# Reordering the first two and last three images, and moving one accumulation bank from the maxima to the first products

## The chip, the cores and the metric

The kernel runs on one core of a Trainium2 chip. Its engines are TensorE (PE: matmuls, and PEld: its weight loads), VectorE (DVE), ScalarE (ACT), GpSimd (POOL) and SyncE (SP: DMA issue). Each runs its own stream of instructions in order, and they meet at semaphores. The metric is the device time in microseconds (us), a median over runs; lower is better. Accumulation memory has eight banks, each holding 128 x 512 float32 values. The kernel uses all eight.

## The reference, cut to what matters

The input is x, 8 images of 32 x 32 positions with 96 channels. For each image, 1024 tokens of 96 values:

```
x = x + moe_a(groupnorm(x))            # 8 experts, hidden 384, gates = softmax over the top 2 of 8
t = x + attention(layernorm(x))        # 6 heads of 16, causal, over all 1024 tokens, with projection
out = t + moe_c(layernorm(t))          # 4 experts, hidden 384, top 2 of 4, gates renormalised
```

Both mixtures compute every expert for every token: h = gelu(x @ W1[e] + b1[e]), y = h @ W2[e], and the sum of gate[e] * y + b2.

## The kernel before, in words

**Splitting.** Float32 operands are cut into a high and a low float16 half, and a product is three matmuls (high x high, low x high, high x low). Weights are scaled by 64 and cut once, at the start, in six parts of two experts each (`split_w1`, `split_w2`, lines 1215 to 1224): VectorE writes the high half and then the low one (`split`, line 1059). The same function cuts the gate's and the attention weights.

**Groups and slots.** A group is one expert on one chunk of 512 tokens: 16 groups for the first mixture of an image (2 chunks x 8 experts), 8 groups for the last one. A group has four slots. In slots 0 to 2 TensorE multiplies the chunk with a third of W1 into a bank `ps_u` (`first_layer`, nine matmuls in three slots); ScalarE applies gelu twice, to float32 `hid` and to float16 `hidh` (lines 951, 952); GpSimd subtracts and writes the low half `hidl` (line 637). One group later, TensorE multiplies by W2 into a bank `ps_y` (`second_layer`, one block of 128 tokens a slot), and VectorE combines with the gates into `acc`, four instructions at a time (`combine`, line 1133). There are two banks `ps_u` and two banks `ps_y`. A first product waits until ScalarE has read the bank that it writes: `h_ready` at all but one of the products before (line 711).

**Attention.** The rows' maxima are found first. For each head and block of 128 queries there are one or two score products into the banks `ps_r`, of which there are three, and a VectorE reduction of each (`maximum`, lines 790 and 1178); 72 of them per image. A score product waits until the reduction three before is done (line 798). Then the maxima are transposed, cut into halves and written by DMA as extra rows of q (`maxima`), and in the softmax stage of 24 steps TensorE computes the transposed scores again with the maximum subtracted, into the five banks `ps_r` and `ps_u` in turn, ScalarE exponentiates, GpSimd clears the future on the diagonal, and TensorE multiplies with the values. Sums of rows go through DRAM by DMA and come back spread over partitions (`rb`), which VectorE multiplies into `yt`.

**Iterations.** Iteration `it` runs, in this order on every engine, the groups of image `it`'s first mixture (phase 0), the groups of image `it - 2`'s last mixture (phase 1), and image `it - 1`'s softmax (phase 2). `schedule(it)` places all other work, called chores, by phase and slot: loading and normalising the next image (`x_load`, `x_turn`, `gn_*`), the routing (`logits`, `exp`, `route`, `gates`, `bias`), the maxima (`max`), and the chain behind attention (`sum_inverse`, `normalise_y`, `project`, `ln2`, `x2_turn`). All engines walk the same table, each doing its own part of a chore; a chore stands in its engine's queue ahead of what follows it.

Iterations 2 to 7 have all three parts. Iterations 0 and 1 have no last mixture, and 0 no softmax. Iteration 8 has no groups: it runs the 72 maxima of image 7 in the slots of phase 0, with nothing beside them but the end of image 6's attention, and then image 7's softmax. Iteration 9 runs the last mixture of image 6, iteration 10 that of image 7. In full iterations 56 of the maxima lie in phase 0 and 16 in phase 1.

**The start.** GpSimd sets all constants (lines 564 to 593) and raises `zeroed`, for which VectorE's first instruction (line 1212), the first group mean and SyncE's remaining weight loads wait. The group-normalised operand of every image is `xah`, `xal`; so image 1's can be written only after image 0's last first product.

Of the kernel before, what the change touches and what calls it, by code (L numbers as in the profile page):

```python
# [26 lines left out]
P = 128  # L27
NIMG, T, D = 8, 1024, 96
TT = T // P
CH = 512  # L30
# [50 lines left out]
def walk(iteration):  # L81

    for it in range(FIRST_LOOP):
        iteration(it, True, it >= 1, it >= 2)
    for it in range(FIRST_LOOP, NIMG):
        iteration(it, True, True, True)
# [5 lines left out]
def image_c(it):  # L92

    return Image(it, -3 if isinstance(it, int) and it > NIMG else -2)
# [61 lines left out]
def maxima_at(first, last, n0, n1):  # L156
# [11 lines left out]
ROUTE_C_LATE = [(0, "route_c", 0), (0, "route_c", 1), (1, "route_c", 2), (1, "route_c", 3), (4, "gates_c", 0),  # L168
                (5, "bias_c", 0), (6, "bias_c", 1)]
# [5 lines left out]
              (10, "gates_a", 0), (20, "bias_a", 0), (22, "bias_a", 1), *FRONT)  # L175
MAX_A = 56


def schedule(it):

    if isinstance(it, int) and it == 0:
        first = [(0, "split_w2", 0), (1, "route_a", 0, 0), (1, "route_a", 1, 0), (1, "route_a", 2, 0),
                 (2, "split_w1", 1), (3, "gates_a", 0, 0), (4, "bias_a", 0, 0), (5, "bias_a", 1, 0),
                 (6, "split_w2", 1), (7, "x_load", 0)]
        first += [(8 + 2 * n, ("split_w1", "split_w2")[n % 2], 2 + n // 2) for n in range(2 * W1_PARTS - 4)]
        first += [(25 + n, "turn_watt", n) for n in range(3)] + [(29 + n, "turn_wp", n) for n in range(2)]
        first += [(32 + 2 * n, "zero", n) for n in range(ZEROS)]
        return placed(*first, *GN), placed((0, "gn_apply", 0)), placed()
    if isinstance(it, int) and it == 1:

        first = [(0, "logits_a", 0, 0), (0, "exp_a", 0, 0), (1, "route_a", 0, 0), (1, "route_a", 1, 0),
                 (2, "route_a", 2, 0), (4, "gates_a", 0, 0), (5, "bias_a", 0, 0), (6, "bias_a", 1, 0),
                 (7, "ln1", 0, -1), (8, "ln1", 1, -1), (8, "x_load", 0), (11, "ln1_apply", 0, -1),
                 (12, "ln1_apply", 1, -1)]
        first += [(14 + 2 * n, "x1_turn", n, -1) for n in range(NC)] + [(18 + 2 * n, "qk", n, -1) for n in range(2 * NC)]
        return (placed(*first, (26, "val", 0), (28, "val", 1), (29, "keep_x1", 0),
                       *maxima_at(32, SLOTS_A - 1, 0, MAXU), *GN),
                placed(*GN_LATE, (3, "maxima", 0)), SOFT)
    if isinstance(it, int) and it == NIMG:

        return (placed(*VALUES, (16, "sum_inverse", 0), (34, "normalise_y", 0), (35, "normalise_y", 1),
                       (37, "project", 0), (40, "project", 1), (41, "keep_x1", 0),
                       *maxima_at(3, SLOTS_A - 1, 0, MAXU)),
                placed((0, "maxima", 0)),
                placed((0, "ln2", 0), (1, "ln2", 1), (4, "ln2_apply", 0), (5, "ln2_apply", 1), (6, "x2_turn", 0),
                       (8, "x2_turn", 1), (11, "logits_c", 0), (12, "exp_c", 0), (13, "route_c", 0),
                       (14, "route_c", 1), (15, "route_c", 2), (16, "route_c", 3), (21, "gates_c", 0)))
    if isinstance(it, int) and it == NIMG + 1:

        return (placed(),  # L210
                placed((1, "bias_c", 0, -3), (4, "bias_c", 1, -3), (5, "sum_inverse", 0), (14, "normalise_y", 0),
                       (15, "normalise_y", 1), (16, "project", 0), (18, "project", 1), (19, "ln2", 0),
                       (20, "ln2", 1), (25, "ln2_apply", 0), (26, "ln2_apply", 1), (28, "x2_turn", 0),
                       (30, "x2_turn", 1)),
                placed((0, "store", 0, -3)))
    if isinstance(it, int) and it == NIMG + 2:

        return (placed(),
                placed((0, "logits_c", 0, -3), (0, "exp_c", 0, -3),
                       *((slot, name, unit, -3) for slot, name, unit in ROUTE_C_LATE)),  # L220
                placed((0, "store", 0, -3)))
# [7 lines left out]
PROLOGUE = ["split_gate", "x_turn", "x_turn", "gn_stats", "gn_mean", "gn_spread", "split_w1", "gn_apply", "logits_a",  # L229
            "exp_a"]  # L230
# [9 lines left out]
Group = namedtuple("Group", "moe c e")  # L240


def rounds(moe_a, moe_c):

    groups = [Group(0, c, e) for c in range(NC) for e in range(EA)] * moe_a
    groups += [Group(1, c, e) for c in range(NC) for e in range(EC)] * moe_c
    if not moe_a:  # L250
        yield None, None, 0, range(SLOTS_A)
    for n, (up, down) in enumerate(zip(groups + [None], [None] + groups) if groups else ()):
        phase, g = (0, n) if moe_a and n < GA + (not moe_c) else (1, n - GA * moe_a)
        yield up, down, phase, range(TC * g, TC * (g + 1))
    if not moe_c:
        yield None, None, 1, range(SLOTS_C)
# [10 lines left out]
def prologue(m, chore):  # L267

    for n, name in enumerate(PROLOGUE):
        run_chores(m, chore, [(name, n - 1 if name == "x_turn" else 0, Image(0, 0))])  # L270
# [7 lines left out]
def build(nc, x, cWg, cbg, cW1, cb1, cW2, cb2, w_attn, b_attn, w_proj, b_proj,  # L278
          fWg, fbg, fW1, fb1, fW2, fb2, out):
    nc.disable_value_cache = True  # L280
    with ExitStack() as ctx:
# [109 lines left out]
        ps_u = [ctx.enter_context(nc.psum_tensor(f"ps_u{i}", [P, CH], F32)) for i in range(2)]  # L391
        ps_y = [ctx.enter_context(nc.psum_tensor(f"ps_y{i}", [P, CH], F32)) for i in range(2)]
        ps_r = [ctx.enter_context(nc.psum_tensor(f"ps_r{i}", [P, CH], F32)) for i in range(3)]
        ps_m = ctx.enter_context(nc.psum_tensor("ps_m", [P, CH], F32))

        def operand_c(b):

            last = isinstance(b.value(1, 0), int) and b.value(1, 0) == NIMG - 1
            return (xah, xal) if last else (xch, xcl)
# [12 lines left out]
        zeroed = sem("zeroed")  # L412
        zeroed_late = sem("zeroed_late")
        consts = sem("consts")
        ident_ready = sem("ident_ready")
        wg_ready = sem("wg_ready")
        w1_ready = sem("w1_ready")
# [41 lines left out]
        def _(sp):  # L459
# [26 lines left out]
            for part in range(2, W1_PARTS):  # L486
                load_w1(part)
                load_w2(part)
            sp.dma_start(watt[:], w_attn.rearrange("(s o) i -> o s i", s=3)).then_inc(watt_loaded, 16)
# [57 lines left out]
            def iteration(it, moe_a, attend, moe_c):  # L547
                for _, _, phase, slots in rounds(moe_a, moe_c):
# [12 lines left out]
        def _(pool):  # L561
# [9 lines left out]
            for tile, value in ((epsilon, 1e-5), (power, -0.5), (minus, -1.0), (ra.gates, 0.0), (rc_.gates, 0.0),  # L571
                                (rc_.prob, -1.0), (b2a, 0.0), (b2c, 0.0), (wpad, 0.0)):
                g.memset(tile[:], value)
            pool.drain()
            for tile, value in ((identb, 0.0), (mask_q, 0.0), (mpart, NEG), (mtop, 0.0)):
                g.memset(tile[:], value)
            pool.drain()
            for tile, value in ((xah, 1.0), (xal, 0.0), (xbh, 1.0), (xbl, 0.0), (xch, 1.0), (xcl, 0.0)):
                g.memset(tile[ONE:ONE + 1, :], value)
# [7 lines left out]
                            pattern=[[3, D // 3], [0, 3]], channel_multiplier=-1)  # L587
            pool.drain().then_inc(zeroed, 1)
            g.affine_select(out=identb[:], in_=identb[:], compare_op=ALU.not_equal, fill=1.0, base=0,
                            pattern=[[-1, P]], channel_multiplier=1)  # L590
            g.affine_select(out=mask_q[:], in_=mask_q[:], compare_op=ALU.is_ge, fill=NEG, base=0,
                            pattern=[[-1, P]], channel_multiplier=1)
            pool.drain().then_inc(consts, 1)
# [36 lines left out]
            def iteration(it, moe_a, attend, moe_c):  # L630
                for up, _, phase, slots in rounds(moe_a, moe_c):
# [17 lines left out]
            for name in PROLOGUE:  # L649
                chore(name, 0, Image(0, 0))  # L650
# [3 lines left out]
        def _(pe):  # L654
# [52 lines left out]
            def first_layer(it, group, j):  # L707

                xh, xl = (xah, xal) if group.moe == 0 else operand_c(image_c(it))
# [4 lines left out]
                bank = ps_u[(HT * grp.k + j) % 2]  # L714
# [666 lines left out]
```

## Time and profile before

| | us |
|---|---|
| Median of 3 runs | 1399.39 (1399.3 to 1401.2) |
| The profiled execution | 1401.64 |
| Its span, first to last instruction | 1399.8 |
| TensorE busy | 1254.4 (90%) |
| ScalarE busy | 983.0 (70%) |
| VectorE busy | 824.3 (59%) |
| GpSimd busy | 796.7 (57%) |

Busy times are unions over the whole span, and a share near 90% is an average over stages that differ. Matmuls overlap in the pipeline, so busy does not mean that TensorE is at its peak. The granted clock (PEclk) is the share of full speed; its two levels are 1.2 and 2.4 GHz.

### The profile page before, as it was taken

The numbers are of one execution on the slowest core, as the hardware profiler recorded it, in microseconds if no ns is written. First come the engines' busy times: TensorE is split into PE (matmuls) and PEld (weight loads), VectorE is DVE, ScalarE is ACT, GpSimd is POOL, SyncE is SP. The second block draws the span as 40 slices with busy tenths as digits, with TensorE's granted clock in tenths as the row PEclk, the third lists the DMA queues.
The fourth block names the chain that finished last, engine by engine and source line by source line (L and its number), as shares of the span: only waits on it lengthen the run. The fifth ranks groups of instructions, "written<-read, shape, count | busy, mean of one in ns | idle before, by whom it ended". The sixth has DMA issues, their size and how long they took to land.

```text
span 1399.8 us, 32907 instructions
## 1 busy us (share of the span) xinstructions
PE 1254.4 (90%) x12573; PEld 726.5 (52%) x12573; DVE 824.3 (59%) x2526; ACT 983.0 (70%) x2008; POOL 796.7 (57%) x815
## 2 busy tenths in 40 slices
PE   3797896999999999999999999999999999998868
PEld 1464553366644665366645665366644665342445
DVE  4865386178834787178834787178834774383342
ACT  2575755867787778877787778867787778606666
POOL 4675553277835676277835676276835676102556
PEclk9887998999999999999999999999999999958988
DMA  5000300310013000310013000310003000210100
GB/s 119 12 2 13 58 1 2 66 28 2 2 29 77 2 2 14 69 25 2 2 31 75 2 2 14 69 25 2 2 28 67 2 2 14 57 24 2 25 12 13
DMA packets 38159, 34.77 MB, mean 25 GB/s; under 512 B 26859, under 2 KB 28780, under 8 KB 38002
## 3 DMA queue, kind: packets, MB, share of 16 engines
q1 hardware_dynamic: 21362, 26.37, 8.9%
q10 hardware_dynamic: 16640, 6.29, 1.7%
q8 instruction: 100, 1.64, 0.5%
q14 instruction: 57, 0.47, 0.1%
HBM read 22.62 MB, written 9.63 MB: 23 GB/s over the span
## 4 chain that ended last, share of the span: by engine, by line
PE 56%; DVE 18%; ACT 8%; issue 7%; POOL 4%; SPq 2%; DMA 2%; POOLq 2%; DVEq 1%; ACTq 0%
PE ps_y L658 21%; PE ps_u L658 18%; PE ps_r L658 9%; PE ps_m L658 7%; DVE mpart L1184 4%; POOL hidl L637 3%; DVE acc L1133 3%; ACT hidh L952 3%; ACT xn L966 2%; DVE yt L1312 2%; ACT hid L951 1%; POOLq L617 1%; SPq L529 1%; PE ps_m L677 1%; SPq L513 1%
## 5 line engine op out<-in xcount | busy, mean ns | idle before, releaser
L637 POOL TENSOR_TENSOR hidl<-hid,hidh 128x512 f16<-128x512 f32 x576 | 679.5, 1195 | 267.7 <-ACT hidh L952 259.5
L951 ACT ACTIVATE hid<-ps_u 128x512 f32<-128x512 f32 x576 | 343.7, 597 | 264.2 <-PE ps_u L658 250.0
L658 PEld LDWEIGHTS ps_y<-w2s,hidh 128*128 128x128 f16 x4608 | 277.0, 98 | 152.3 <-issue 15.0
L952 ACT ACTIVATE hidh<-ps_u 128x512 f16<-128x512 f32 x576 | 341.7, 593 | 0.0
L1184 DVE TENSOR_REDUCE mpart<-ps_r 128x1 f32<-128x512 f32 (+2 forms) x576 | 296.6, 548 | 73.6 <-PE ps_r L658 64.5
L658 PE MATMUL ps_y<-w2s,hidh 128*128 128x96 f16 x4608 | 324.1, 207 | 7.8 <-DVE acc L1133 7.8
L599 POOL TENSOR_SCALAR_AFFINE_SELECT probs<-probs 128x384 f32<-128x384 f32 x128 | 66.5, 521 | 296.2 <-ACT probs L991 296.1
L658 PE MATMUL ps_y<-w2s,hidl 128*128 128x96 f16 x2304 | 226.7, 208 | 4.8 <-POOL hidl L637 4.0
L658 PE MATMUL ps_r<-ks,qs 96*128 96x512 f16 (+2 forms) x576 | 193.8, 351 | 16.3 <-DVE mpart L1184 8.1
L658 PE MATMUL ps_u<-xah,w1h 97*128 97x512 f16 x408 | 161.8, 397 | 34.8 <-ACT hidh L952 29.8
L991 ACT ACTIVATE probs<-ps_r 128x512 f32<-128x512 f32 (+3 forms) x352 | 152.7, 510 | 29.2 <-PE ps_r L658 29.1
L658 PE MATMUL ps_y<-probs,vaug 128*32 128x512 f32 (+3 forms) x1152 | 161.4, 499 | 0.8 <-POOL probs L599 0.5
L658 PE MATMUL ps_u<-xah,w1l 97*128 97x512 f16 x408 | 160.1, 392 | 0.0
L658 PE MATMUL ps_u<-xal,w1h 97*128 97x512 f16 x408 | 160.0, 392 | 0.0
L658 PEld LDWEIGHTS ps_y<-w2s,hidl 128*128 128x128 f16 x2304 | 142.3, 99 | 6.4 <-POOL hidl L637 6.3
L991 ACT ACTIVATE probs<-ps_u 128x512 f32<-128x512 f32 (+3 forms) x224 | 104.2, 522 | 20.5 <-PE ps_u L658 11.7
L1133 DVE SCALAR_TENSOR_TENSOR acc<-ps_y,gatesa,acc 128x96 f32<-128x96 f32 x448 | 110.2, 308 | 10.9 <-PE ps_y L658 8.4
L658 PE MATMUL ps_r<-qs,ks 98*128 98x512 f16 (+3 forms) x352 | 92.0, 334 | 7.7 <-DMA qs<-mtl 7.2
L658 PE MATMUL ps_r<-mask_q,identb 128*128 128x128 bf16 x384 | 88.0, 231 | 0.0
L658 PEld LDWEIGHTS ps_r<-ks,qs 96*128 96x128 f16 x576 | 58.2, 102 | 46.3 <-DVE mpart L1184 37.0
L658 PE MATMUL ps_u<-xch,w1h 97*128 97x512 f16 x168 | 64.5, 384 | 10.0 <-ACT hidh L952 8.6
L658 PEld LDWEIGHTS ps_u<-xah,w1h 97*128 97x128 f16 x408 | 41.5, 102 | 61.5 <-ACT hidh L952 47.2
(185 smaller groups left out, 1462.1 us busy)
## 6 DMA issues: line engine op xcount, KB each, us to landing
rb<-rsum_dram SPq DMA_DIRECT2D x24, 256.0 KB, 4.2
qs<-qk_dram SPq DMA_DIRECT2D x48, 96.0 KB, 3.0
ks<-qk_dram SPq DMA_DIRECT2D x48, 96.0 KB, 3.9
xin<-in_x_dram ACTq DMA_DIRECT2D x8, 384.0 KB, 3.7
qk_dram<-qk_h SPq DMA_DIRECT2D x16, 192.0 KB, 2.1
qk_dram<-qk_l SPq DMA_DIRECT2D x16, 192.0 KB, 2.3
out_dram<-xo ACTq DMA_DIRECT2D x8, 384.0 KB, 2.9
w_raw<-in_L_conv_W_dram SPq DMA_DIRECT2D x8, 288.0 KB, 4.4
```

The costliest lines, as they stand in the source:

```text
L513: sp.dma_start(dst[HD * n:HD * (n + 1), heads, :], qk_dram[part, s, heads.start * HD:heads.stop * HD, :] .rearrange("(h d) t -> d h t", h= ...
L529: sp.dma_start(sums[n:n + TT, :], yt[32 * g + HD:32 * g + HD + 1, t, :] .rearrange("a (i q) -> a i q", q=P)).then_inc(sums_in, 16)
L599: g.affine_select(out=block, in_=block, compare_op=ALU.is_ge, fill=0.0, base=0, pattern=[[0, TR], [1, P]], channel_multiplier=-1).then_inc ...
L637: g.tensor_tensor(hidl[:, grp.k % HB, j, :], hid[:, j, :], hidh[:, grp.k % HB, j, :], ALU.subtract).then_inc(hl_ready, 1)
L658: return nc.tensor.matmul(dst, lhsT, rhs, start=start, stop=stop, skip_group_check=True)
L951: a.activation(hid[:, j, :], bank[:], ACT.Gelu, scale=1.0 / WS)
L952: a.activation(hidh[:, grp.k % HB, j, :], bank[:], ACT.Gelu, scale=1.0 / WS).then_inc(h_ready, 1)
L966: last = a.activation(dst[:, t, :], src[:, t, :], ACT.Identity, bias=shift[:, t:t + 1], scale=rstd[:, t:t + 1])
L991: a.activation(probs[:, n % 3, g, 0:w], soft_bank(k)[:, 0:w], ACT.Exp, scale=float(HD) ** -0.5).then_inc(p_ready, 1)
L1133: last = v.scalar_tensor_tensor(out=out[:, t, :], in0=ps_y[grp.k % 2][:, D * i:D * (i + 1)], scalar=r.gates[:, t, e:e + 1], in1=acc[:, t, ...
L1184: v.tensor_reduce(mpart[:, h, i, part:part + 1], ps_r[k % 3][:, 0:w], AX, ALU.max).then_inc(mx_free, 1)
L1312: v.tensor_tensor(yt[:, k, :], yt[:, k, :], rb[:, k, :], ALU.mult).then_inc(yn_ready, 1)
```

## The change

The order of the first two and last three images is another one, some work changes engine, and one bank moves.

- **Banks.** `ps_u` has three banks and `ps_r` two. A first product waits for the gelu three before it, a maximum's score for the reduction two before it. The softmax uses the same five banks in turn. `ps_y` and `ps_m` are as before.
- **Start.** GpSimd sets the group matrix's constants first (`group_ready`), then those that the gate's split and the b2 loads need (`zeroed`), and the rest after the prologue (`constants()`, `padded`, `consts`). The group statistics come before `split_gate` and `split_w1`. The high halves of all W1 and W2 parts are written by ScalarE, the low ones still by VectorE.
- **Iteration 0.** The weight parts and the attention weights lie in later slots, the memset of the mask rows is cut in three parts. Image 1's group norm and gate logits are done in slots 60 and 63, into `xch`, `xcl` (`operand_a`), which are first needed in iteration 2.
- **Iteration 1.** Everything before the maxima is earlier; they take slots 27 to 63 and not 32 to 63. After the last group come only the maxima and layer norm statistics; group norm, logits and layer norm's application of the next image are in the softmax (`SOFT_LATE`).
- **Iteration 7** has no last mixture: 72 maxima beside its 16 groups, then the softmax. **Iteration 8** runs image 5's last mixture, with the 72 maxima of image 7 in slots 2 to 33. **Iteration 9** runs the last mixtures of images 6 and 7 as 16 groups in one, with image 7's chain from the sums to the gates in slots 4 to 42. There is no iteration 10.
- Iterations 2 to 6 have the same chores in the same slots as before.

```diff
-    for it in range(FIRST_LOOP):
-        iteration(it, True, it >= 1, it >= 2)
...
-    iteration(NIMG, False, True, False)
-    iteration(NIMG + 1, False, False, True)
-    iteration(NIMG + 2, False, False, True)
+    for it in range(NIMG + 2):
+        iteration(it, 1 <= it <= NIMG)
...
+    if it == NIMG:
+        return (placed(),
+                placed((0, "val", 0), (1, "bias_c", 0, -3), (3, "val", 1), (6, "bias_c", 1, -3), (7, "sum_inverse", 0),
+                       (14, "normalise_y", 0), (15, "normalise_y", 1), (17, "project", 0), (19, "project", 1),
+                       (20, "keep_x1", 0), *maxima_at(2, 33, 0, MAXU), (33, "maxima", 0)),
...
+    if it == NIMG + 1:
+        return (placed(),
+                placed((0, "bias_c", 0, -3), (2, "bias_c", 1, -3), (4, "sum_inverse", 0), (13, "normalise_y", 0),
+                       (14, "normalise_y", 1), (16, "project", 0), (18, "project", 1), (19, "ln2", 0), (20, "ln2", 1),
+                       (23, "ln2_apply", 0), (24, "ln2_apply", 1), (26, "x2_turn", 0), (28, "x2_turn", 1),
+                       (30, "logits_c", 0), (31, "exp_c", 0), (32, "route_c", 0), (33, "route_c", 1),
+                       (34, "route_c", 2), (38, "route_c", 3), (38, "store", 0, -3), (39, "gates_c", 0),
+                       (40, "bias_c", 0), (42, "bias_c", 1)),
...
+    first = [Group(0, c, e, it) for c in range(NC) for e in range(EA)] if it < NIMG else []
+    if it == NIMG + 1:
+        return first, dense(NIMG - 2, range(NC)) + dense(NIMG - 1, range(NC))
+    if it == NIMG:
+        return first, dense(NIMG - 3, range(NC))
+    return first, dense(it - 2, range(NC)) if 2 <= it < NIMG - 1 else []
...
-        ps_u = [ctx.enter_context(nc.psum_tensor(f"ps_u{i}", [P, CH], F32)) for i in range(2)]
+        ps_u = [ctx.enter_context(nc.psum_tensor(f"ps_u{i}", [P, CH], F32)) for i in range(3)]
...
-        ps_r = [ctx.enter_context(nc.psum_tensor(f"ps_r{i}", [P, CH], F32)) for i in range(3)]
+        ps_r = [ctx.enter_context(nc.psum_tensor(f"ps_r{i}", [P, CH], F32)) for i in range(2)]
...
+        def operand_a(b):
+            return (xch, xcl) if b.value(1, 0) == 1 else (xah, xal)
...
-                wait(pe, h_ready, grp.value(HT, j - 1))
+                wait(pe, h_ready, grp.value(HT, j + 1 - len(ps_u)))
...
-                wait(pe, mx_free, b.value(MAXU, k - 2))
+                wait(pe, mx_free, b.value(MAXU, k + 1 - len(ps_r)))
...
+                if name == "split_w1":
+                    act.wait_ge(w1_loaded[k], 32)
+                    w = slice(2 * HID * k, 2 * HID * (k + 1))
+                    a.activation(w1h[:, w], w1_raw[:, w], ACT.Copy, scale=WS).then_inc(w1_high, 1)
...
                 if name == "split_w1":
-                    dve.wait_ge(w1_loaded[k], 32)
+                    dve.wait_ge(w1_high, k + 1)
                     w = slice(2 * HID * k, 2 * HID * (k + 1))
-                    split(w1h[:, w], w1l[:, w], w1_raw[:, w], WS)
+                    v.scalar_tensor_tensor(out=w1l[:, w], in0=w1_raw[:, w], scalar=WS, in1=w1h[:, w], op0=ALU.mult,
+                                           op1=ALU.subtract)
                     dve.drain().then_inc(w1_ready, 1)
```

## Rows read from the trace of the kernel before

**Rows 1.** Windows: PE, PEld, DVE, ACT, POOL busy us; clock; DMA share.
```profile
21.50:117.30 95.80, 74.24 (x747) 47.18 (x745) 68.78 (x154) 53.77 (x100) 59.66 (x50) 0.86 0.08 16
117.30:233.80 116.50, 91.92 (x951) 57.87 (x952) 74.14 (x252) 65.75 (x126) 60.15 (x58) 0.88 0.12 22
169.40:217.00 47.60, 44.49 (x455) 27.86 (x453) 40.50 (x102) 25.06 (x46) 24.46 (x22) 0.97 0.06 8
233.80:274.40 40.60, 39.94 (x242) 12.69 (x243) 9.71 (x20) 34.43 (x82) 8.31 (x16) 0.96 0.17 39
589.20:746.70 157.50, 149.51 (x1574) 88.24 (x1572) 98.24 (x310) 122.71 (x252) 98.58 (x98) 1.00 0.10 25
1142.20:1178.00 35.80, 34.01 (x413) 22.99 (x411) 21.14 (x71) 28.40 (x57) 29.74 (x30) 1.00 0.01 2
1218.60:1267.30 48.70, 39.74 (x152) 17.69 (x150) 41.32 (x96) 1.22 (x2) 0.00 (x0) 0.52 0.10 20
1305.80:1399.80 94.00, 73.72 (x798) 49.47 (x793) 35.91 (x132) 57.14 (x110) 57.41 (x52) 0.86 0.08 19
```
**Rows 2.** Waits of PE, 21.5:117.3: total us, times, longest us.
```profile
PE ps_y L658 <- DVE acc L1133: 7.8, 3, 3.1
PE ps_u L658 <- DVE xal L1271: 4.1, 1, 4.1
PE ps_m L691 <- DVE gatesa L1119: 3.6, 1, 3.6
PE ps_m L915 <- DVE wql L1063: 3.3, 2, 2.0
```
**Rows 3.** Timeline of ACT, DVE: start us, us, instruction [idle before].
```profile
7.30 0.59 ACT L1003 ACTIVATE xt<-ps_m 96x512 f32<-96x512 f32 x1 [1.18 <-PE ps_m L677]
...
11.84 0.17 DVE L1061 TENSOR_SCALAR wgh<-wg_raw 97x12 f16<-97x12 f32 x1 [11.84 <-POOLq L588]
...
16.10 0.59 DVE L1061 TENSOR_SCALAR w1h<-w_raw 97x768 f16<-97x768 f32 x1
...
38.82 1.31 DVE L1061 TENSOR_SCALAR w1h<-w_raw 97x768 f16<-97x768 f32 x1
```
**Rows 4.** Waits of PE, 117.3:233.8.
```profile
PE ps_u L658 <- ACT hidh L952: 4.5, 2, 2.5
```
**Rows 5.** Timeline of PE and DVE, end of stage 1.
```profile
216.69 0.38 PE L658 MATMUL ps_u<-xal,w1h 97*128 97x512 f16 x1
...
222.06 0.99 DVE L1133 SCALAR_TENSOR_TENSOR x<-ps_y,gatesa,acc 128x96 f32<-128x96 f32 x4 [0.27 <-PE ps_y L658]
...
229.41 0.25 DVE L1190 TENSOR_REDUCE mtop<-mpart 128x48 f32<-128x96 f32 x1
...
233.76 1.46 PE L658 MATMUL ps_r<-qs,ks 98*128 98x512 f16 x3 [3.56 <-DMA qs<-mtl]
```
**Rows 6.** Waits of PE, the steady stage 589.2:746.7.
```profile
PE ps_u L658 <- ACT hidh L952: 4.7, 5, 1.4
PE ps_m L691 <- DVE gatesc L1119: 0.7, 1, 0.7
PE ps_r L658 <- DVE mpart L1184: 0.5, 2, 0.3
```
**Rows 7.** Timeline of PE and DVE, routing in a steady stage.
```profile
650.36 0.38 PE L658 MATMUL ps_r<-ks,qs 96*128 96x512 f16 x1
650.59 0.38 PE L658 MATMUL ps_u<-xah,w1h 97*128 97x512 f16 x1
...
652.33 0.55 DVE L1184 TENSOR_REDUCE mpart<-ps_r 128x1 f32<-128x384 f32 x1
```
**Rows 8.** Line 1040 by source (durations in ns), and ACT's timeline.
```profile
L1040 ACT ACTIVATE x1r<-x x8: 842/846/848, 162.6 to 1248.3; 128x768 f32<-128x768 f32 x8
...
231.00 2.97 ACT L966 ACTIVATE xn<-x,shift,rstd 128x96 f32<-128x96 f32 x8 [12.81 <-POOL shift L618]
```
**Rows 9.** Waits of PE, 1305.8:1399.8.
```profile
PE ps_u L658 <- ACT hidh L952: 5.6, 5, 3.1
```

More of the change, by code:

```diff
@@ L181, in schedule @@
     if isinstance(it, int) and it == 0:
[L182 to L186, printed above, removed]
@@ L199, in schedule @@
[L199 to L207, printed above, removed]
@@ new lines, in schedule @@
+        first += [(15 + 3 * n, ("split_w1", "split_w2")[n % 2], 3 + n // 2) for n in range(2 * W1_PARTS - 6)]
+        first += [(34, "turn_watt", 0), (37, "turn_watt", 1), (41, "turn_watt", 2), (44, "turn_wp", 0),
+                  (46, "turn_wp", 1)]
+        first += [(33 + 4 * n, "zero", n) for n in range(ZEROS)]
+        return (placed(*first, (39, "x_turn", 0), (43, "x_turn", 1), (51, "gn_stats", 0), (54, "gn_mean", 0),
+                       (57, "gn_spread", 0), (60, "gn_apply", 0), (63, "logits_a", 0)),
+                placed((0, "ln1", 0, 0), (0, "ln1", 1, 0), (1, "route_a", 0), (1, "route_a", 1)), placed())
@@ new lines, in schedule @@
+    if isinstance(it, int) and it == 1:
+        first = [(1, "exp_a", 0, 0), (2, "route_a", 2, 0), (4, "ln1_apply", 0, -1), (5, "ln1_apply", 1, -1),
+                 (6, "gates_a", 0, 0), (7, "bias_a", 0, 0), (8, "bias_a", 1, 0), (9, "x_load", 0),
+                 (10, "x1_turn", 0, -1), (12, "x1_turn", 1, -1)]
+        first += [(14 + 2 * n, "qk", n, -1) for n in range(2 * NC)]
+        return (placed(*first, (22, "val", 0), (24, "val", 1), (25, "keep_x1", 0),
+                       *maxima_at(27, SLOTS_A - 1, 0, MAXU), *GN),
+                placed((0, "maxima", 0), (1, "ln1", 0), (1, "ln1", 1)), SOFT_LATE)
@@ L237, in chores, with groups_of, dense, rounds @@
             yield name, unit, Image(it, off or 0)
[L240 to L250, printed above, removed]
-        yield None, None, 0, range(SLOTS_A)
[L252 to L255, printed above, removed]
+Group = namedtuple("Group", "moe c e b")
+def groups_of(it):
+    def dense(b, cs):
+        return [Group(1, c, e, b) for c in cs for e in range(EC)]
+    first = [Group(0, c, e, it) for c in range(NC) for e in range(EA)] if it < NIMG else []
[4 more added lines that the diff above has]
+    return first, dense(it - 2, range(NC)) if 2 <= it < NIMG - 1 else []
+def rounds(it):
+    first, second = groups_of(it)
+    groups = first + second
+    if not first:
+        yield None, None, 0, range(SLOTS_A)
+    for n, (up, down) in enumerate(zip(groups + [None], [None] + groups)):
+        late = second and n >= len(first)
+        g = n - len(first) if late else n
+        yield up, down, 1 if late else 0, range(TC * g, TC * (g + 1))
+    if not second:
         yield None, None, 1, range(SLOTS_C)
@@ L570, in _ @@
             g.iota(expert[:], pattern=[[0, TT], [1, 8]], base=0, channel_multiplier=0)
[L571 to L579, printed above, removed]
+            g.memset(epsilon[:], 1e-5)
+            g.memset(power[:], -0.5)
             pool.drain()
@@ L647, in iteration @@
                         chore(name, k, b)
-            for name in PROLOGUE:
-                chore(name, 0, Image(0, 0))
+            for name, unit in PROLOGUE:
+                chore(name, unit, Image(0, 0))
+            constants()
             walk(iteration)
@@ L739, in moes @@
                 older = None
-                if moe_a:
+                if it < NIMG:
                     pe.wait_ge(xt_free, Image(it, 0).value(1, 1))
-                for up, down, phase, slots in rounds(moe_a, moe_c):
+                for up, down, phase, slots in rounds(it):
                     if starts and up and up.c == 0 and up.e % 2 == 0:
@@ L1137, in combine, with combined, moes @@
                 grp.k += 1
-            def combined(it, group):
+            def combined(group):
                 last = group.e == (EA, EC)[group.moe] - 1
                 if last and group.c == 0 and group.moe == 0:
-                    wait(dve, x1r_ready, Image(it, 0).value(1, 0))
+                    wait(dve, x1r_ready, group.b)
                 if last and group.c == 0 and group.moe == 1:
-                    wait(dve, out_done, image_c(it).value(16, 0))
+                    wait(dve, out_done, 16 * group.b)
                 combine(group, (x1, xo)[group.moe] if last else acc)
-            def moes(it, moe_a, moe_c):
+                if last and group.c == NC - 1 and group.moe == 1:
+                    dve.drain().then_inc(xo_ready, 1)
+            def moes(it):
                 older = None
-                for up, down, phase, slots in rounds(moe_a, moe_c):
+                for up, down, phase, slots in rounds(it):
                     for slot in slots:
```

162 lines of the change are left out of this document (85 added, 77 removed).

## The prediction

> **What bounds the kernel now.** Read the stages first, because the change treats them differently. In the busy times by window [rows 1] a steady stage (589.2 to 746.7 us: one image's first mixture, another's last one, a third's attention) has TensorE busy 149.51 of 157.50 us at granted clock 1.00; five such stages follow one another up to 1062 us. ScalarE has 122.71 there, VectorE 98.24, GpSimd 98.58. The steady part is TensorE's, with about 8 us in it that could be won. The ends are another thing. The first mixture (21.5 to 117.3) has TensorE busy 74.24 of 95.80 us, at a mean clock of 0.86. The stage from 1218.6 to 1267.3 holds the 72 score maxima of the last image and no mixture: TensorE's clock is 0.52 there (nearly all of it at 1.2 GHz, after 1.00 before it), VectorE has 41.32 of 48.70 us, GpSimd nothing. The last two mixtures alone take 94.0 us for 73.72 busy. For comparison, 8 groups of a last mixture with 16 maxima beside them take 35.80 us at full clock (1142.2 to 1178).
>
> Then the waits of TensorE say who holds it. In the first mixture it is VectorE, which cuts the weights into high and low halves (7.8 us; the name is that of its last instruction before them), writes the next image's operand (4.1), routes (3.6) and turns the attention weights (3.3) [rows 2]. In the second stage ScalarE has 4.5 us [rows 4], beside q and k on their way through DRAM. In a steady stage it is ScalarE, 4.7 us in 5 waits, and VectorE's maxima hardly at all, 0.5 us [rows 6].
>
> **The change part by part.** Terms are against the profiled execution, 1401.64 us with a span of 1399.8; it lies 2.25 us above the median of 1399.39. Negative is gain.
>
> (1) Start. VectorE's first instruction, the gate's split, waits for all of GpSimd's constants until 11.84 us, and the group statistics stand behind it; what they read, the turned image, is there at 7.30 + 0.59 = 7.89 [rows 3]. They now go first and wait only for the group matrix's constants. 11.84 - 7.89, and 0.5 for the split's two instructions: -4.4. The high half of w1 leaves VectorE (-0.6), the split comes in behind the statistics (+0.5). -4.5; below nothing is excluded, as nothing is put ahead of the statistics, and more than -5.5 too, as the image has to come.
>
> (2) First mixture. Eleven weight parts remain to be cut in two. The high half costs VectorE 0.59 us where GpSimd is idle and 1.31 us beside it [rows 3]: up to 14 us leave VectorE. ScalarE takes eleven times at most 0.85, the price of its 128x768 copy [rows 8], so 9 us on top of 53.77 of 95.80. Waits that go: 7.8 for the halves and for the memset of the mask rows, now in three parts; 3.3 for the attention weights, turned later; 4.1 for the operand, since image 1 gets the pair of buffers that is free until stage 2; 2 of the 3.6 for routing. 17.2 in all. The time at 1.2 GHz shrinks a little with them (-2), and a shorter distance from the group spread to the operand costs 1. -18 leaves 78 us, over ScalarE's 54 + 9 and table loads. Bounds: -10, if ScalarE comes late at each part, to -24, if the clock stays up.
> The Trainium skill, SBUF — State Buffer, section Who interferes with whom, says that VectorE's two-port forms contend with GpSimd, and that ScalarE never waits on anyone. The doubling in rows 3 agrees. By that rule ScalarE pays each high half once; the sum is the same by the rule and by the row, as the row's 0.85 was taken once.
>
> (3) Second stage. Before the maxima: they begin five slots earlier, a group and a quarter, at (35.8 - 16 x 0.23) / 8 = 4.0 us a group [rows 1, 7] (-5); ScalarE's 4.5 us [rows 4] shrink to 1.5, since routing is half done by then, the layer norm starts before, and a third bank is there (-3); some of the time at 1.2 GHz goes with the empty start (the stage's clock is 0.88 [rows 1]; -5); only seven slots and not eight then cover the way of q and k through DRAM (+1.2). The maxima share 37 slots and not 32: +5 for the work moved in among them, +3 for two banks where VectorE has 40.50 and TensorE 44.49 of 47.60 us [rows 1]. At the end, the last combine is over at 223.05 (222.06 + 0.99), but mtop comes at 229.41, behind the group norm, layer norm and scores of the next image; these move behind it: -6.3 [rows 5]. Sum -10, bounds -3 to -20. In the softmax behind it ScalarE has 34.43 of 40.60 us and a chain through TensorE and back at each step, so the 2.97 us of layer norm moved into it [rows 8] count in full: +3, or 0 if they fit into its gaps.
>
> (4) Five steady stages. The third bank covers ScalarE's absences: 4.7 us of waits, the longest 1.4 [rows 6], which is about one slot. It can give back up to 5; I take 4.5. The two banks for the maxima work against it. VectorE goes off to route and is back at the maxima at 652.33; TensorE meanwhile issues its own side of them, one at 650.36, which with two banks would wait for the reduce that ends at 652.88 [rows 7]. That is 2.5 us, less 0.7 for the gates [rows 6], which then are ready, and 0.3 for a short wait behind them: 1.5. Layer norm, the two products with yt, the routing and the next operand take VectorE away in the same way, five places. Bounds: 0.5, if most fall on waits that stand there anyway, to 12, five times the full 2.5. I take 4.5, near the row's net price for each and some small ones. Net 0, bounds -4 to +7.5 a stage.
>
> (5) Stage 7, now without a last mixture: -35.8 [rows 1]. Its first mixture takes 16 more maxima; the product after one starts 0.23 us later (650.36 to 650.59 [rows 7]), with the mask's a little more: +4.3, and +3 for two banks. The end, which the 8 groups had covered, lies open. Stage 1 shows it: from the last first product, about 217, over the combine, 223.05, and then from mtop to the first score, 229.41 to 233.76: 6.1 + 4.4 = 10.5 [rows 5]. Layer norm in the softmax: +3. Sum -15, bounds -10 to -20.
>
> (6) Stage 8 gets those 8 groups beside the 72 maxima. VectorE: 41.3 as now, 8 times four combines of 0.99 together [rows 5] = 8, bias and a slower yt beside GpSimd 3: 52. TensorE: the 35.8 us of stage 7's last mixture, which has 16 maxima in it, 56 more at 0.23 = 13, projection and values 4: 53. Two engines about equally loaded, coupled through two banks, with the open end of the maxima: 61 for 48.7, +12.3. Bounds: 55, one engine alone, to 68: in stage 1 eight groups and most of the 72 maxima took 47.6 us with three banks [rows 1], and 10.5 for the end, projection, values and more waiting come on top.
>
> (7) Both last mixtures in one run of 16 groups, so that image 7's layer norm and routing pass beside image 6's groups. Of ScalarE's 5.6 us of waits [rows 9] and the routing's, a little less, about 6 go together, and 2 of clock. The wait for yt stays, since its DMA chain is not moved. -8, bounds -3 to -14.
>
> Sum: -4.5 - 18 - 10 + 3 + 0 - 15 + 12.3 - 8 = -40.2. 1401.6 - 40.2 = 1361.4, and at the level of the median 1359.
>
> **The rivals.** (a) The third bank gives more than the second of the maxima cost: net -3.5 in each of six first mixtures, 1359 - 21 = 1338. For it: ScalarE is the first name in rows 6. Against it: rows 7. (b) Two banks cost 4 us net in each: 1383. (c) Stage 8 takes 68 us and the run of 16 groups gains nothing: 1359 + 7 + 8 = 1374. VectorE's 41.32 of 48.70 speaks for it. (d) Slower than before: each of VectorE's absences goes to TensorE in full, 12 us a stage, and the third bank finds nothing to cover, because ScalarE catches up in those waits. 6 x 12 = 72, 1431. It turns the sign from 40.2 / 6 = 6.7 us net a stage on. Against it: the one absence that is worked out nets 1.5. (e) The many small waits on two banks bring TensorE's clock down inside the steady stages. In the first mixture a mean clock of 0.86 means (1 - 0.86) x 2 = 28% of the time at 1.2 GHz; the same in five stages would be 44 us each at half speed, half of them lost, 1359 + 110 = 1469. Against it: clock 1.00 in the steady stage with 8 us idle.
> The Trainium skill, TensorE: Matmul & The Clock Gate, section A second HAM failure mode: psum-queue depth-cycling, describes (e): a kernel that cycles through accumulation banks idles so often that its clock swings. This trace has a low clock only where idle time is large [rows 1].
> (f) The reordering moves waits and removes none, since the same engine is late next: within 0.2%.
>
> **How the numbers follow.** Forecast (1344 to 1376) 0.58; (a) 0.12; (b) 0.13; (c) 0.09; (d) 0.04; (e) 0.02; (f) 0.02. About 0.2% is what a measurement of this kernel can tell from no change. Faster: forecast, a, b, c = 0.92; same 0.02; slower 0.06. The range takes in most of (b), (c) and the near part of (a): 1336 to 1386.
>
> **What would show it.** In the changed profile: the first product of the mixture at about 17 us; stage 1 begins near 95, its softmax near 201; five stages of 157.5 +- 2 us in which TensorE's waits for ScalarE are near zero and those for the maxima have grown to 4 us or more; no stretch at clock 0.52 at the end, but a stage of about 61 us with VectorE over 85% busy; a last run of about 86 us. It would be wrong if a steady stage were over 162 or under 153 us, if the first mixture stayed over 88 (ScalarE then is the new bound), or if stage 8 went over 70.

## The result and the profile after

The changed kernel takes 1419.65 us (median of 4 runs, 1411.2 to 1430.5) against 1399.35 us: ratio 1.0153, 95% interval 1.0117 to 1.0189. Slower, where 1359 us was forecast. The profiled execution has a span of 1420.0 us. One run in this document, of 1438.1 us, is over 1.5% above the fastest of its kernel and is left out of medians, ratios and intervals.

Stages are numbered by iteration. Stages 2 to 6, the steady ones, and stage 7 are given with their softmax, stages 1 and 8 up to its beginning. The windows of the changed kernel, by its own stage boundaries (start:end, length, busy us and instruction counts of PE, PEld, DVE, ACT, POOL, then clock, DMA share, GB/s): first mixture, stage 1, three of the five steady stages, stages 7 and 8, the last run.

```profile
17.10:97.20 80.10, 69.73 (x771) 44.79 (x769) 59.17 (x145) 60.60 (x112) 63.42 (x54) 0.98 0.09 18
97.20:205.90 108.70, 87.97 (x905) 56.18 (x902) 70.19 (x224) 64.43 (x119) 58.16 (x55) 0.93 0.12 23
583.10:747.20 164.10, 153.08 (x1575) 90.07 (x1572) 98.51 (x310) 122.31 (x252) 98.70 (x98) 0.98 0.10 24
747.20:909.10 161.90, 151.36 (x1574) 89.45 (x1571) 98.41 (x310) 122.28 (x252) 98.71 (x98) 0.99 0.11 24
416.40:583.10 166.70, 156.15 (x1575) 91.37 (x1573) 98.49 (x310) 122.39 (x252) 98.70 (x98) 0.96 0.10 23
1074.70:1215.90 141.20, 125.71 (x1169) 68.37 (x1166) 75.81 (x228) 95.85 (x201) 68.45 (x72) 0.93 0.09 21
1215.90:1291.00 75.10, 63.42 (x544) 40.10 (x541) 51.32 (x119) 27.88 (x52) 28.34 (x24) 0.86 0.09 19
1332.20:1420.00 87.80, 70.20 (x796) 48.65 (x793) 35.38 (x132) 56.69 (x110) 58.36 (x52) 0.93 0.08 20
```

The start and the end are what they were meant to be: the first mixture takes 80.1 us where it took 95.8 at clock 0.86, the last run 87.8 where it took 94.0 [rows 1]. The loss sits in the steady stages, whose chores nobody touched. They take 165.6, 166.7, 164.1, 161.9 and 165.6 us in place of 157.0 to 158.3, and their clock is no longer 1.00. The longer the stage, the lower the clock: 161.9 us at 0.99, 166.7 at 0.96. VectorE, ScalarE and GpSimd are as busy in them as before. Stage 8 takes 75.1 us at 0.86.

TensorE's waits in one steady stage (total us, times, longest us), which answer to rows 6:

```profile
PE ps_r L683 <- DVE mpart L1216: 8.1, 7, 2.4
PE ps_y L683 <- POOL hidl L661: 0.8, 3, 0.3
PE ps_m L683 <- DVE yt L1349: 0.6, 1, 0.6
```

The waits for ScalarE's gelu, 4.7 us, are gone, as forecast; those for the maxima's reductions went from 0.5 to 8.1. But the stage is 6.6 us longer, and only 3.0 of it is idle time of TensorE (164.10 - 153.08 = 11.0 us against 157.50 - 149.51 = 8.0). The other 3.6 us are busy time, with the same instructions. The timeline of PE in the same stage shows where they come from. The columns are start, us, instruction, and idle before:

```profile
684.28 0.29 PE L683 MATMUL ps_y<-w2s,hidl 128*128 128x96 f16 x3
686.65 0.39 PE L683 MATMUL ps_r<-ks,qs 96*128 96x512 f16 x1 [2.07 <-DVE mpart L1216]
...
687.15 0.38 PE L683 MATMUL ps_u<-xch,w1l 97*128 97x512 f16 x1
687.37 0.38 PE L683 MATMUL ps_u<-xcl,w1h 97*128 97x512 f16 x1
...
690.10 0.63 PE L683 MATMUL ps_u<-xch,w1h 97*128 97x512 f16 x1
690.53 0.63 PE L683 MATMUL ps_u<-xch,w1l 97*128 97x512 f16 x1
```

After a wait of 2.07 us the products of 512 columns follow one another 0.22 us apart, and 3 us later 0.43 us apart: the clock is at 1.2 GHz for some products, without any idle time between them. Such products count as busy, so this loss stands in no list of waits; the clock column, the distance of starts and a busy time that grew at equal work show it. Over the five steady stages TensorE is idle for 54.4 us in place of 40.6 and busy for 769.5 in place of 747.0. Of the 36.3 us that they lose, 13.8 are so waits and 22.5 the clock.

### The profile page after: what moved, and what is told of

Read it like the earlier page. It is cut to its first block, busy times and chain, and to the rows that moved or that the text cites. A ratio compares the mean times of both kernels' runs of the same rounds, so it can differ in the third digit from the quotient of the medians.

```text
span 1420.0 us, 32919 instructions
## 1 busy us (share of the span) xinstructions
PE 1269.9 (89%) x12573; PEld 737.1 (52%) x12573; DVE 814.2 (57%) x2517; ACT 992.3 (70%) x2024; POOL 802.5 (57%) x815
## 4 chain that ended last, share of the span: by engine, by line
PE 55%; DVE 19%; ACT 8%; issue 6%; SPq 3%; DMA 3%; POOL 3%; DVEq 2%; POOLq 0%; ACTq 0%
PE ps_y L683 20%; PE ps_u L683 18%; PE ps_r L683 9%; PE ps_m L683 7%; DVE mpart L1216 5%; DVE acc L1165 3%; POOL hidl L661 3%; ACT hidh L976 2%; ACT hid L975 2%; ACT xn L990 2%; SPq L545 2%; DVE yt L1349 2%; SPq L529 1%; DMA sums<-yt 1%; DMA qs<-mtl 1%
## 5 line engine op out<-in xcount | busy, mean ns | idle before, releaser
L1216 DVE TENSOR_REDUCE mpart<-ps_r 128x1 f32<-128x512 f32 (+2 forms) x576 | 302.7, 550 | 120.4 <-PE ps_r L683 111.3
L1015 ACT ACTIVATE probs<-ps_u 128x512 f32<-128x512 f32 (+1 forms) x336 | 152.2, 524 | 24.3 <-PE ps_u L683 16.3
L683 PE MATMUL ps_u<-xah,w1h 97*128 97x512 f16 x360 | 142.3, 395 | 1.6 <-ACT hidh L976 1.6
L683 PE MATMUL ps_u<-xal,w1h 97*128 97x512 f16 x360 | 141.7, 394 | 0.0
L683 PE MATMUL ps_u<-xah,w1l 97*128 97x512 f16 x360 | 141.5, 393 | 0.0
L1015 ACT ACTIVATE probs<-ps_r 128x512 f32<-128x512 f32 (+3 forms) x240 | 107.0, 500 | 16.8 <-PE ps_r L683 16.5
L683 PE MATMUL ps_u<-qs,ks 98*128 98x512 f16 (+1 forms) x336 | 92.1, 341 | 2.0 <-ACT probs L1015 1.4
L683 PE MATMUL ps_u<-xch,w1h 97*128 97x512 f16 x216 | 86.4, 400 | 3.3 <-ACT hidh L976 3.3
L683 PE MATMUL ps_u<-xcl,w1h 97*128 97x512 f16 x216 | 86.6, 401 | 0.0
L683 PE MATMUL ps_u<-xch,w1l 97*128 97x512 f16 x216 | 86.2, 399 | 0.0
```

Source lines behind the costliest of these rows:

```text
L683: return nc.tensor.matmul(dst, lhsT, rhs, start=start, stop=stop, skip_group_check=True)
L1015: a.activation(probs[:, n % 3, g, 0:w], soft_bank(k)[:, 0:w], ACT.Exp, scale=float(HD) ** -0.5).then_inc(p_ready, 1)
L1216: v.tensor_reduce(mpart[:, h, i, part:part + 1], ps_r[k % len(ps_r)][:, 0:w], AX, ALU.max).then_inc(mx_free, 1)
```

## The experiments

Names say how many banks the first products (u) and the maxima (r) have. "order" is the changed kernel's order and chores.

**New order, old banks.**

```diff
-        ps_u = [... for i in range(3)]
+        ps_u = [... for i in range(2)]
-        ps_r = [... for i in range(2)]
+        ps_r = [... for i in range(3)]
```

> The changed kernel with the banks of before: two for the first products, three for the maxima. Theory A (the bank that moved is the loss, through waits for the maxima's reductions and the dips of TensorE's clock that they bring): five steady stages of 157.5 us at clock 1.00 in place of 161.9 to 166.7, stage 8 in 62 to 66 in place of 75, so 1420 - 36 - 10 = about 1372, and below 1380 in any case. Rival B (the new order is the loss, above all stage 8 with two engines equally loaded): at least 1405, with stage 8 over 72 us.

Measured: 1363.22 us (1361.3 to 1369.6), 0.9746 of before, interval 0.9710 to 0.9783. Second time, on one chip with the changed kernel: 1366.0 us, 0.9751 (0.9727 to 0.9775).

> New order with the old banks, beside them: 1360 to 1366 us, spread under 8 us; stages of 157.5 us.

Its windows, stage for stage with those above (one steady stage):

```profile
17.20:97.40 80.20, 70.48 (x773) 45.04 (x771) 58.93 (x145) 60.81 (x112) 63.42 (x54) 0.98 0.09 18
97.40:201.80 104.40, 86.75 (x906) 55.56 (x902) 69.31 (x224) 64.43 (x119) 58.20 (x55) 0.93 0.12 24
561.90:719.50 157.60, 149.44 (x1574) 88.22 (x1571) 98.38 (x310) 122.68 (x252) 98.55 (x98) 1.00 0.10 25
1035.00:1168.30 133.30, 120.08 (x1169) 65.76 (x1167) 74.87 (x228) 96.03 (x201) 68.86 (x72) 0.96 0.10 22
1168.30:1229.60 61.30, 52.54 (x545) 35.02 (x542) 49.61 (x119) 27.64 (x52) 28.41 (x24) 0.97 0.12 23
1270.80:1361.50 90.70, 71.95 (x796) 49.42 (x793) 35.02 (x132) 57.26 (x110) 57.40 (x52) 0.92 0.08 19
```

This settles which part of the change did it. Rival B falls: the new order with the old banks is 2.5% faster than before, and all of the loss came with the bank. (Theory A's 1372 us had left out stage 7 and part of stage 8.) Between the two profiled spans, 1420.0 and 1361.5, lie 58.5 us: 3.5 up to the end of stage 1's softmax, 36.2 in the five steady stages, 7.9 in stage 7, 13.8 in stage 8 with its softmax, and -2.9 in the last run, the one place where the third bank helps.

**Old order, new banks.** The same ranges in the kernel before, and the waits with them:

```diff
...
-                wait(pe, h_ready, grp.value(HT, j - 1))
+                wait(pe, h_ready, grp.value(HT, j + 1 - len(ps_u)))
...
-                wait(pe, mx_free, b.value(MAXU, k - 2))
+                wait(pe, mx_free, b.value(MAXU, k + 1 - len(ps_r)))
...
```

> The kernel before, in its own order, with three banks for the first products and two for the maxima. Theory A: each of the six full stages (274 to 1218 us) grows by 5 to 9 us, the clock falls below 1.00 in them, stage 1 grows by 2 or 3: 1399 + 45 + 3 = about 1445. Rival B: the banks are neutral, 1395 to 1405.

Measured: 1454.9 us (1453.8 to 1459.1), 1.0389 (1.0363 to 1.0414), above even what theory A asked for. The bank costs 54 us here and 56 in the new order. A steady stage has the same signature, 8.5 us of waits for the maxima and a clock of 0.98:

```profile
612.40:776.70 164.30, 152.96 (x1574) 90.52 (x1571) 98.53 (x310) 122.24 (x252) 98.66 (x98) 0.98 0.09 24
PE ps_r L658 <- DVE mpart L1184: 8.5, 7, 2.5
```

**The two halves of the bank move apart.** Two banks for each, the eighth in the softmax only:

```diff
-        ps_u = [... for i in range(3)]
+        ps_u = [... for i in range(2)]
+        ps_x = ctx.enter_context(nc.psum_tensor("ps_x", [P, CH], F32))
...
-        soft_banks = ps_r + ps_u
+        soft_banks = ps_r + [ps_x] + ps_u
...
```

> The changed kernel with two banks for the first products and two for the maxima; the eighth bank serves only the softmax, which keeps its five. It prices the two halves of the bank move apart. If the third bank for first products gives back the 4.7 us a stage that TensorE had waited for ScalarE, this kernel is 15 to 25 us slower than the changed one, 1435 to 1445. If ScalarE catches up in the waits for the maxima anyway (the third bank finds nothing to cover), it is within 5 us of the changed one, 1415 to 1425.

> Two banks for first products, two for maxima, beside the changed kernel on the same chip. If the third bank for first products is worth nothing where the maxima have two: within 0.3% of the changed kernel, or faster. If it gives back the 4.7 us a stage: slower by 15 us or more.

> The changed kernel once more, on one chip with the next three, so that they can be set against each other: 1412 to 1425 us. Its runs should spread wider than those of the kernels with three banks for the maxima, since stage 8 takes 66 or 75 us according to where TensorE's clock falls.

Measured first: 1416.36 us, 1.0123 (1.0094 to 1.0152), so within 5 us of the changed kernel. Then side by side on one chip, in 12 and 5 runs: 1408.37 us, 1.0056 (1.0031 to 1.0081), against 1419.8 us, 1.0141 (1.0111 to 1.0170), for the changed kernel. The intervals are apart. Where the maxima have two banks, the third bank for first products costs some 12 us and brings nothing. A steady stage says why:

```profile
576.00:739.30 163.30, 151.81 (x1574) 89.26 (x1571) 98.66 (x310) 122.58 (x252) 98.66 (x98) 0.99 0.10 24
PE ps_r L684 <- DVE mpart L1217: 5.7, 7, 2.4
PE ps_u L684 <- ACT hidh L977: 3.7, 4, 1.4
```

With two banks for first products the waits are 5.7 us for the maxima and 3.7 for ScalarE, 9.4 in all; with three they are 8.1 for the maxima and 0.8 for GpSimd, 8.9. TensorE, no longer held by ScalarE, arrives earlier at the same reductions of VectorE and waits there. What is saved in many small waits comes back in the large ones, and the changed kernel's stages pay for those with clock: its second profile has all five at 166.5 to 169.0 us, here they are 161.5 to 167.4 over two profiles. As expected the changed kernel spreads wide, 1415 to 1438 with the run that is left out; but not for the reason given. Stage 8 took 75 us in both of its profiles. It is here, with two and two banks, that stage 8 was 66.4 and 68.0 us long.

**Filling a wait.** As the kernel with two and two banks, with nine products (`FILL`) into the free bank, ahead of the wait behind the routing, in the five steady stages:

```diff
+                if k == 40 and 1 <= b.value(1, 0) < NIMG - 2:
+                    for _ in range(FILL):
+                        mm(ps_x[:], w1h[:, 0:P], xah[:, 0:CH])
                 wait(pe, mx_free, b.value(MAXU, k + 1 - len(ps_r)))
```

> As order_u2r2 (2 and 2 banks, the eighth free outside the softmax), with nine products of 512 columns into the free bank, whose result nobody reads, just ahead of the one long wait of each full stage, that for the maxima's reduction behind the routing (2.4 us); 9 x 0.22 = 2.0 us of it are so filled. The wait's length to the outside stays the same. If TensorE's clock falls because of that wait, the dip about 63 us into each of the stages goes and each is 1.7 to 3.4 us shorter: 1405 to 1411 against 1416. If the waits alone are the loss and the dips cost nothing: 1416 to 1420, with the dips where they were.

Measured: 1403.48 us (12 runs, 1398.6 to 1408.4), 1.0037 (1.0017 to 1.0057), against 1.0123 and 1.0056 for the same kernel without them. Against the first of these the intervals are apart, against the second they overlap. The profile is clearer: the five stages take 162.1, 161.3, 161.5, 161.2 and 161.9 us where they took 163.7, 163.0, 163.3, 163.1 and 167.4, and every one of them is at 1.00. Work that nobody needs, put into a wait, made four of the stages 1.6 to 1.9 us shorter. The fifth, 5.5 us shorter, had fallen a second time in the kernel without the fill, 9 us in and away from the filled wait. That kernel's second profile has one stage without a fall, and it takes 161.5 us, as with the fill: the 2 us are the fall's. Two windows, a steady stage and stage 8:

```profile
574.70:736.20 161.50, 152.30 (x1585) 89.05 (x1582) 98.56 (x310) 122.65 (x252) 98.69 (x98) 1.00 0.11 24
1199.60:1274.60 75.00, 63.37 (x544) 40.14 (x541) 51.31 (x119) 27.87 (x52) 28.33 (x24) 0.86 0.10 19
```

and stage 8 of the kernel without the fill, which has the same instructions there:

```profile
1210.40:1276.80 66.40, 53.96 (x544) 33.66 (x541) 51.09 (x120) 27.75 (x52) 28.35 (x24) 1.00 0.12 21
```

The same stage costs 66 or 75 us by whether TensorE's clock fell in it (1.00 or 0.86), at the same work of VectorE (51.1 and 51.3 us busy). So of the 13.8 us that the changed kernel loses there, about 9 are the clock and 5 the waits. Why it falls in one and not in the other is open: up to the fall, 29 us in, the waits of the two agree to 0.01 us. The changed kernel falls at the same place, and its waits for the maxima in stage 8, too, are none over 1.4 us:

```profile
PE ps_r L683 <- DVE mpart L1216: 7.0, 17, 1.4
```

**Moving the maxima away from VectorE's absences**, in the full stages, with the changed kernel's banks. The new last argument names slots that get no maxima:

```diff
...
-                   *maxima_at(3, SLOTS_A - 1, 0, MAX_A)),
-            placed(*beside_c, *maxima_at(7, 24, MAX_A, MAXU), ...
+                   *maxima_at(7, SLOTS_A - 1, 0, MAX_A, (45, 46, 47))),
+            placed(*beside_c, *maxima_at(7, 25, MAX_A, MAXU, (13, 14, 15, 16)), ...
```

> The changed kernel, its banks kept; only in the five full stages the maxima avoid the slots in which VectorE is away: they begin in slot 7 and not 3 (VectorE then waits for the sums' DMA), leave out 45 to 47 (routing) and, in the last mixture's part, 13 to 16 (the next operand). Theory A: the waits of 2.2 to 2.6 us go, the clock stays at or near 1.00, a stage falls from 165 to 156 to 159 us: 1375 to 1390. If instead the coupling of two engines through two banks is the loss everywhere and not at single places: 1410 to 1420.

Measured: 1403.64 us (10 runs), 1.0024 (1.0001 to 1.0047), between the two expectations. Then, besides:

```diff
-ROUTE_C = [..., (45, "route_c", 3), (48, "gates_c", 0)]
+ROUTE_C = [..., (45, "route_c", 3), (51, "gates_c", 0)]
-            placed(*beside_c, *maxima_at(7, 25, MAX_A, MAXU, (13, 14, 15, 16)), ...
+            placed(*beside_c, *maxima_at(6, 24, MAX_A, MAXU, (13, 14, 15, 16)), ...
```

> As moved_u3r2 (three banks for first products, two for maxima), and besides the gates' turn goes from slot 48 to 51, where TensorE had taken up a wait of 2.6 us for the routing once the maxima were out of its way, and the last maxima end a slot earlier, ahead of their transpose. If the loss is made of single long absences of VectorE, this takes the last long one: stages of 157 to 159 us at clock 1.00, in all 1380 to 1390. If TensorE, relieved in one place, waits in the next (VectorE's work up to each slot is the limit): 1398 to 1405.

Measured: 1392.46 us (6 runs), 0.9961 (0.9934 to 0.9987). The waits of the first, and of the second, one steady stage each:

```profile
PE ps_r L684 <- DVE mpart L1217: 2.8, 5, 0.8
PE ps_m L717 <- DVE gatesc L1152: 2.6, 1, 2.6
```

```profile
PE ps_r L684 <- DVE mpart L1217: 4.0, 7, 0.9
PE ps_y L684 <- DVE acc L1166: 2.2, 1, 2.2
```

The maxima's waits fall from 8.1 to 2.8 and 4.0 us, but one wait of 2 to 3 us for VectorE stays: first for the gates, then, when these are moved, for the combine, both behind the same routing. The likely reason, not tested apart, is that TensorE is through sooner in three slots without maxima and meets VectorE's next product. Of the second pair of expectations neither time was met, but single places matter: some 27 of 56 us come back by a table of slots. The five steady stages now take 159.1 to 160.8 us, 800 in sum against 788 with three banks for the maxima and 824 in the changed kernel. More is left in stages 7 and 8, whose maxima were not moved: 6.5 and 13.6 us above the kernel with three banks.

The one long wait of each stage is here the same in all five, and the clock falls behind it in some only. In the first of these kernels it is 2.6 us long; three stages fall, and two stay at 1.00, this one of them:

```profile
895.30:1055.60 160.30, 149.81 (x1574) 88.39 (x1571) 98.43 (x310) 122.25 (x252) 98.18 (x98) 1.00 0.11 24
PE ps_m L717 <- DVE gatesc L1152: 2.6, 1, 2.6
```

**A third bank where there are no maxima.**

```diff
+        def up_bank(it, k):
+            banks = ps_u + [ps_r[0]] if it in (0, NIMG + 1) else ps_u
+            return banks[k % len(banks)]
```

> As order_u2r3, and one of the three banks of the maxima serves as a third one for first products in the first stage and in the last, where there are no maxima. The third bank then costs nothing. The waits for ScalarE in the last run (5.0 us) go as in the changed kernel (0.3), where that stage took 87.8 against 90.7 us: 1363 - 2 to -4 = 1360. If TensorE waits for the same routing anyway: 1363.

Measured: 1365.85 us, 0.9764 (0.9739 to 0.9790); the same as without it, so the gain of 2 to 4 us did not come. The waits for ScalarE in the last run go, and those for VectorE's operand and the routing grow from 1.1 and 3.4 to 2.9 and 4.0 us.

**ScalarE's layer norm in two pieces, three slots apart.**

```diff
-TO_C = [(27, "ln2_apply", 0), (28, "ln2_apply", 1), ...
+TO_C = [(26, "ln2_apply", 0), (29, "ln2_apply", 1), ...
-                (11, "ln1_apply", 1), ...
+                (13, "ln1_apply", 1), ...
```

> As late3_u2r3, and the two halves of ScalarE's layer norm are three slots apart instead of one (slots 26 and 29, and 10 and 13), so that two banks last through each. Of 4.7 us a stage for ScalarE about 1.5 go, times six: 1360 - 9 = 1351. If ScalarE's line is only late in another place: 1358 to 1362.

> As order_u2r3, and only the two halves of ScalarE's layer norm are three slots apart; no third bank anywhere. The trace of spread_u2r3 had 3.3 in place of 4.7 us of waits for ScalarE and stages of 157 us: 2 to 6 us below order_u2r3. If there was nothing in it: within 1 us.

Measured: 1361.66 us with the third bank of the experiment before (0.9744, 0.9717 to 0.9771), 1361.81 us without it (0.9718, 0.9697 to 0.9740), beside 1366.0 us and 0.9751 (0.9727 to 0.9775) on the same chip. The intervals overlap a little; the stages are 156.5 to 158.2 us against 157.0 to 158.7 in the profile, 786.0 in sum against 788.7, with 3.3 us of waits for ScalarE in place of 4.7. Probably 3 or 4 us, within the 2 to 6 of the second expectation and below the 9 of the first, and not settled. It is the fastest version here, 2.8% below the kernel before.

## Why the prediction was wrong

By its steps, the profiled spans against each other.

(1) Start: right. First product at 17.1 us, -4.4.

(2) First mixture: 80.1 us, -15.7 for -18; the waits went as listed, but a new one of 2.4 us stands at the group spread, where +1 had been set. ScalarE's price for a high half, "at most 0.85", was 0.92 us for W1 and 0.72 for W2, 8.9 us in all for the 9 set. The cheap price of VectorE's high half, 0.59 us at 16.10, was not taken beside an idle GpSimd, as the prediction has it, but beside one at work on 96 x 1 values; the dear one, 1.31 us, is beside its 128 x 512 subtraction.

(3) Stage 1: -7.8 for -10; with three banks for the maxima it would have been -12.1. Two banks cost 4.3 there, not 3. The softmax behind it grew by 4.3 us and not 3.

(4) **Five steady stages: the step that failed.** Net 0 a stage was forecast, with bounds of -4 to +7.5. Measured is +7.3 on average (823.9 against 787.6 us over five), at the very edge, and above it in the second profile of this kernel (837.4). That a steady stage is over 162 us had been named as a sign of being wrong, and stage 8 over 70 too; both came. Two things in the step were wrong.

First, the third bank's gain. 4.5 us of gain and 4.5 us of loss were set against each other as if they were independent. The loss by two banks for the maxima is near its forecast when taken alone: their waits go from 0.5 to 5.7 us, and ScalarE's from 4.7 to 3.7. The third bank for first products then takes away ScalarE's 3.7 and brings 2.4 for the maxima and 0.8 for GpSimd: 0.5 us are won, not 4.5. That was in the text as a half of rival (d), with 0.04.

Second, the clock, put at nothing. It costs more than the waits, 22.5 us against 13.8 over the five. That was rival (e), with 0.02, turned down because the clock was 1.00 with 8 us idle in a stage. But no single wait in those 8 us is over 1.4 us; the new ones are 1.6 to 3.0. In the 70 steady stages of all profiles, the kernel before included, the clock fell 53 times, and each fall began within 2 us of the end of a wait of 1.6 us or more. There are 66 such waits. Behind those up to 1.5 us there is no fall. The sum of idle time does not sort the stages: one with 9.3 us fell (the last wait of 2.2 us above), one with 9.7 us did not (the filled kernel). So in a steady stage the length of one wait was the thing to look at. It is not the whole rule, as stage 8 fell behind a wait of 1.4 us. (e)'s price, 22 us a stage, was far too high, since it took the clock of the first mixture, where TensorE starves, for the whole stage; measured are 2 to 7 us, 4.5 on average. What happened is neither rival alone but the two mechanisms together, each at a part of its price.

The Trainium skill, TensorE: Matmul & The Clock Gate, section A second HAM failure mode: psum-queue depth-cycling, tells of another kernel that cycles through accumulation banks: TensorE idles for short times between groups of matmuls, often enough to make its clock swing between its two levels. The trace agrees in that the clock falls behind TensorE's waits for a bank (0.96 to 0.99 in the stages above), and the fill shows that without the wait it does not. That it is their number, the steady stages do not bear out: with five waits for ScalarE of up to 1.4 us they stay at 1.00. Nor is the clock low only where idle time is large, as the prediction read rows 1: the window 233.8 to 274.4 is at 0.96 with TensorE busy for 39.94 of 40.60 us.

(5) Stage 7: 141.2 us for 156.6, -15.4, and -15 was forecast. Right in sum by luck, from two errors: the bank that moved costs 7.9 us there, not 3, and the rest, 133.3 us without it, had been set too dear by as much.

(6) Stage 8: 75.1 us, forecast 61, bounds 55 to 68. With three banks for the maxima it is 61.3. The sum of the two engines' work was right, the coupling through two banks was not, nor was there anything for the clock. The softmax behind it took 41.2 us for 38.5, for which nothing had been set.

(7) Last run: -6.2 for -8.

With the bank left where it was the kernel takes 1363 us, close to the 1359 forecast. That is in part luck: stage 7 is 8.3 us and stage 1 2.1 us below its term, and the first mixture, the softmaxes of stages 1 and 8 and the last run are 12 us above theirs in sum. The one row about the banks [rows 7] was read rightly (2.5 us, and the trace after has 2.4 there), but priced by its net cost in a stream that did not change otherwise.

## What to carry to other kernels

When a bank or buffer moves from one user to another, look at who sets the pace. The buffer that is nearly never waited for (0.5 us) may be so because it is deep enough to bridge a long absence of a slow partner. The one that is waited for in short pieces (4.7 us in five) may give back little, as the time saved is spent at the next wait. And where two changes come together, time each alone: here one was worth -2.5% and the other +4%, and the sum hid both.

A wait of TensorE can have a second price behind it. Read the clock of the stretch after it, or the distance between equal products, before a stage is called bound by its waits.

## What the runs showed of the hardware

In steady stages, in which TensorE was over 92% busy, 53 of 66 single waits of 1.6 to 3.0 us had a fall of the clock to 1.2 GHz within 2 us of their end, with products of 512 columns at 0.43 in place of 0.22 us and no idle time in between. Waits of the same length did both: of five at 2.6 us (maxima moved once) three had one. In the kernels whose longest wait in such a stage is 1.4 us (three banks for the maxima) the clock stayed at 1.00. Nine useless products in a wait of 2.4 us kept the clock at 1.00 in all five stages and shortened four of them by 1.6 to 1.9 us.

A stage of unchanged instructions took 66.4 us at clock 1.00 and 75.0 us at 0.86 in two kernels that differ only earlier; the fall came behind a wait of 1.4 us, which both have.

The changed kernel's runs go with their clock: 1411 us at a mean of 0.960, 1438 us at 0.942. With three banks for the maxima they lay within 1360 to 1369 us on one chip. Long waits alone do not make the runs differ so: the old order with the new banks has them too, and its four runs lie within 5.3 us.
